# First graph network of a chain: Wm and the two halves of W1 multiplied with each other first, edge sums then on 128 columns

## What is computed

```python
m = max(max(weighting_gate), 0);  exp_e = exp(weighting_gate - m)
row_sum = segment_sum(exp_e, src, num_segments=n_nodes)
atten_e = exp_e / (row_sum[src] + 1e-06)
Mfeat = source_features @ Wm + bm                       # 625 x 512 @ 512 x 256
out0 = segment_sum(atten_e[:, None] * Mfeat[dst], src)  # 625 x 256
out1 = segment_sum(atten_e[:, None] * Mfeat[src], dst)  # 625 x 256
h = concatenate([out0, out1], axis=-1) @ W1 + b1        # 625 x 512 @ 512 x 128
h = relu(layernorm(h, gamma, beta))
h = relu(h @ W2 + b2)                                   # 625 x 128 @ 128 x 512
```

## Time and profile before

| | us |
|---|---|
| median of 3 runs | 2250.25 |
| lowest and highest of them | 2247.23 and 2251.97 |
| the profiled execution, its time | 2255.45 |
| its span, first to last instruction | 2253.6 |
| PE busy | 2119.1 |
| DVE, ACT, POOL busy | 1024.7, 710.9, 551.3 |
| the stretch that the change touches, by PE's rows | 680.7 to 762.1 |

### The profile page before, as it was taken

The page is one execution under the profiler, slowest core; times in us unless marked ns, Lnnn a source line. Parts: engine busy times, 40 slices in busy tenths (PEclk is TensorE's granted clock), DMA queues, the critical chain, the costliest instruction groups (busy, mean ns, idle before and its releaser), DMA issues.

```text
span 2253.6 us, 21932 instructions
## 1 busy us (share of the span) xinstructions
PE 2119.1 (94%) x8162; PEld 1276.7 (57%) x8162; DVE 1024.7 (45%) x2159; ACT 710.9 (32%) x1191; POOL 551.3 (24%) x467
## 2 busy tenths in 40 slices
PE   5899887898889999998999999999999999999998
PEld 3577564787456565554565565565565544444443
DVE  8898677686334324356445355255355300000002
ACT  1477565675231110012242242252251111111110
POOL 4678763453220101012003003002102200122202
PEclk9999999799999789999999999999999899999999
DMA  9522213631112102111011011010101677778832
GB/s 345 178 32 32 27 14 76 171 90 60 41 58 75 38 19 86 43 75 61 15 57 62 19 57 42 30 51 24 53 9 48 246 294 291 295 303 300 300 128 74
DMA packets 61507, 237.47 MB, mean 105 GB/s; under 512 B 23343, under 2 KB 28419, under 8 KB 39276
## 3 DMA queue, kind: packets, MB, share of 16 engines
q1 hardware_dynamic: 31898, 168.25, 20.7%
q0 software_dynamic: 26336, 62.19, 9.0%
q10 hardware_dynamic: 3168, 5.63, 0.7%
HBM read 204.06 MB, written 31.96 MB: 105 GB/s over the span
## 4 chain that ended last, share of the span: by engine, by line
PE 77%; DVE 12%; issue 4%; POOL 3%; ACT 3%; DMA 2%; ACTq 0%; DVEq 0%; POOLq 0%
PE PS L739 10%; PE PS L1027 10%; PE PS L732 9%; PE PS L1420 7%; PE PS L1429 7%; PE PS L1458 7%; PE PS L883 3%; PE PS L1065 3%; PE PS L1306 2%; PE PS L1223 2%; PE PS L1326 2%; PE PS L1327 2%; PE PS L750 1%; PE PS L1205 1%; DVE AR L2436 1%
## 5 line engine op out<-in xcount | busy, mean ns | idle before, releaser
L1984 POOL TENSOR_TENSOR RSTD<-VE,HALF 125x1 f32<-125x1 f32 x100 | 81.1, 811 | 972.5 <-DVE VE L2154 972.5
L1027 PE MATMUL PS<-XT,WR 128*128 128x500 f32 (+2 forms) x992 | 233.5, 392 | 8.4 <-ACT XT L1526 4.4
L883 PE MATMUL PS<-HR,HOT 125*125 125x512 f32 x800 | 211.8, 413 | 16.4 <-DVE HOT L2298 14.9
L2991 DVE TENSOR_TENSOR AR<-AR,PS 128x512 f32<-128x512 f32 (+1 forms) x44 | 30.3, 688 | 404.3 <-PE PS L1429 404.3
L739 PE MATMUL PS<-WR,XT 128*125 128x512 f32 (+1 forms) x464 | 205.5, 590 | 0.6 <-DVE AR L2775 0.3
L1027 PEld LDWEIGHTS PS<-XT,WR 128*128 128x128 f32 x992 | 144.7, 193 | 87.9 <-issue 72.5
L883 PEld LDWEIGHTS PS<-HR,HOT 125*125 125x125 f32 x800 | 147.0, 192 | 58.3 <-DVE HOT L2298 17.2
L2002 POOL DMA_INDIRECT pair_sums<-CW,SIDX x80 | 136.2, 1702 | 54.1 <-DMA pair_sums<-CW,SIDX 21.9
L739 PEld LDWEIGHTS PS<-WR,XT 128*125 128x125 f32 x464 | 86.9, 193 | 89.0 <-issue 85.0
L732 PE MATMUL PS<-XT,WR 128*128 128x313 f32 (+3 forms) x432 | 120.7, 436 | 1.8 <-DVE CW L2262 1.3
L1943 ACT ACTIVATE AR<-PS 128x512 f32<-128x512 f32 (+1 forms) x44 | 26.3, 597 | 299.0 <-PE PS L1420 299.0
(11 more groups left out here) (427 smaller groups left out, 3874.2 us busy)
## 6 DMA issues: line engine op xcount, KB each, us to landing
WR<-in_qkv SPq DMA_DIRECT2D x12, 1024.0 KB
WR<-in_omm SPq DMA_DIRECT2D x12, 1024.0 KB
pair_scores<-CNT SPq DMA_DIRECT2D x1, 12212.0 KB
AR<-pair_scores SPq DMA_DIRECT2D x5, 2187.5 KB
AR<-in_x_a SPq DMA_DIRECT2D x10, 1024.0 KB, 9.8
AR<-in_x_b SPq DMA_DIRECT2D x10, 1024.0 KB, 4.9
AR<-in_x_c SPq DMA_DIRECT2D x10, 1024.0 KB, 7.3
WR<-in_x_a SPq DMA_DIRECT2D x8, 1024.0 KB, 8.9
```

The lines of the kernel that those rows point to most:

```text
L883: last = mm(DIFF[m % 4], HOT[g % 2][0:P, k, tile(j)], HR[0:P, k, :, b, :], start=(k == 0 and b == 0), stop=(k == NT - 1 and b == 1))
L1027: last = mm(by_tile(s)[:, t0:t1, :], w[:, k, 128 * m:128 * (m + 1)], XT[:, k, P * t0:P * t1].rearrange("p (c n) -> p c n", n=P), start=(k ...
L1984: g.tensor_tensor(RSTD[:, t:t + 1], VE[:, t:t + 1], HALF[:, :], ALU.pow)\
```

## The change

Wm and W1 are multiplied with each other before the node features come in: (XT Wm) W1 becomes XT (Wm W1). In part `u` = 2 of the feed-forward network, after the products of `m` = 0, PE turns Wm and the bias row bm (`turn_feature_matrix`, 10 transposes in two W slots). After `m` = 1 it multiplies the turned Wm with both halves of W1 (`joint_weights`): 2 matmuls for the bias row, 8 for the matrix, 256 columns each, in two W slots. ACT copies the four slots to TURNED_WM, JOINT_BIAS and JOINT. `project_narrow` reads JOINT in the place of Wm. The two edge sums are made by node tile, into an N slot for each tile: `hidden_of(t)` is now 10 matmuls of 128 columns with tiles of G and PT as the stationary side and MF moving, and the result stands in node rows. The four turned blocks, their ACT copies and the product with W1 are left out. The product with the noise features (`FW`, 2 matmuls) goes ahead of all `hidden_of`, the waits for the weight batch and for `ROWS` move up into part 2, and DVE waits for JOINT_BIAS before its bias adds.

```diff
+        JOINT = view(XL_, 128, K4, 256)
+        JOINT_BIAS = view(XL_ + K4 * 256, P, 256)
+        TURNED_WM = view(XL_ + K4 * 256 + 256, 128, 2, 640)
...
+            def turn_feature_matrix():
+                weights(0, 3)
+                w_m = WR[:, 0, 0, 0:K4 * 256].rearrange("p (c n) -> p c n", c=K4)
+                pe.wait_ge(rows_in, 16)
+                both = []
+                for k in range(2):
+                    s = fill("W")
+                    for c in range(K4):
+                        nc.tensor.transpose(s.ap[:, 128 * c:128 * (c + 1)], w_m[:, c, 128 * k:128 * (k + 1)], ID[:, :])
+                    nc.tensor.transpose(s.ap[:, D:D + P], ROWS[:, R_BM + 128 * k:R_BM + 128 * (k + 1)], ID[0:P, 0:P])                        .then_inc(s.filled, 1)
+                    both.append((s, n.now(s.filled)))
+                return both
+
+            def joint_weights(turned_wm):
+                w_1 = WR[:, 0, 1, 0:K4 * 128].rearrange("p (c n) -> p c n", c=K4)
+                for half in turned_wm:
+                    copied(half)
+                rows = fill("W")
+                for k in range(2):
+                    last = mm(rows.ap[0:P, 0:256].rearrange("p (a b) -> p a b", a=2),
+                              TURNED_WM[:, k, D:D + P], w_1[:, k::2, :], start=(k == 0), stop=(k == 1))
+                last.then_inc(rows.filled, 1)
+                s = fill("W")
+                for m in range(K4):
+                    for k in range(2):
+                        last = mm(s.ap[:, 256 * m:256 * (m + 1)].rearrange("p (a b) -> p a b", a=2),
+                                  TURNED_WM[:, k, 128 * m:128 * (m + 1)], w_1[:, k::2, :],
+                                  start=(k == 0), stop=(k == 1))
+                last.then_inc(s.filled, 1)
+                return s, n.now(s.filled)
...
+                    if u == 2 and m == 1:
+                        turned_wm = turn_feature_matrix()
+                    if u == m == 2:
+                        joint = joint_weights(turned_wm)
...
+            copied(joint)
             for t in range(NT):
                 copied(turns[t])
-                moved.append(project_narrow(w_m, t, 256))
+                moved.append(project_narrow(JOINT, t, 256))
...
-            sides = [(fill("W"), 2), (fill("W"), 3)]
-            for k in range(NT):
-                pe.wait_ge(moved[k][0].taken, moved[k][1])
-                for s, f in sides:
-                    for c0, c1 in ((0, CUT), (CUT, N)):
-                        last = mm(s.across[0:128, c0:c1], MF[:, k, 128 * (f % 2):128 * (f % 2 + 1)],
-                                  G[:, k, c0:c1], start=(k == 0), stop=(k == NT - 1))
...
-            for f in range(2):
-                s = fill("W")
-                wide(s, 128, NT, lambda k: MF[:, k, 128 * f:128 * (f + 1)], lambda k: PT[:, k, :])
             all_taken("W")
...
-                narrow(s, 128, [(HT[:, f, tile(t)], w_1[:, f, :]) for f in range(4)])
+                terms = [(by[:, k, tile(t)], MF[:, k, 128 * f:128 * (f + 1)], k)
+                         for f, by in ((1, G), (0, PT)) for k in range(NT)]
+                for j, (lhs, rhs, k) in enumerate(terms):
+                    if t == 0 and j < NT:
+                        copied(moved[k])
+                    last = mm(s.ap[0:P, 0:128], lhs, rhs, start=(j == 0), stop=(j == 2 * NT - 1))
+                last.then_inc(s.filled, 1)
```

On ACT the four copies to HT go, and these come:

```diff
+                    if u == 2 and m == 1:
+                        for k in range(2):
+                            s = take("W")
+                            fn(TURNED_WM[:, k, 0:D + P], s.ap[:, 0:D + P], ACT.Copy).then_inc(s.taken, 1)
+                    if u == m == 2:
+                        s = take("W")
+                        fn(JOINT_BIAS, s.ap[0:P, 0:256], ACT.Copy).then_inc(s.taken, 1)
+                        s = take("W")
+                        fn(JOINT[:, :, :], s.ap[:, 0:K4 * 256].rearrange("p (c n) -> p c n", c=K4), ACT.Copy)\
+                            .then_inc(s.taken, 1)
...
-            for f in (2, 3, 0, 1):
-                s = take("W")
-                fn(HT[:, f, :], s.across[:, :], ACT.Copy).then_inc(s.taken, 1)
```

More of the change, by code:

```diff
@@ L1105, in _ @@
                 weights_done()
-            weights(0, 3)
-            w_m = WR[:, 0, 0, 0:K4 * 256].rearrange("p (c n) -> p c n", c=K4)
-            w_1 = WR[:, 0, 1, 0:K4 * 128].rearrange("p (c n) -> p c n", c=K4)
             w_2 = WR[:, 0, 2, 0:D]
             moved = []
+            copied(joint)
             for t in range(NT):
                 copied(turns[t])
-                moved.append(project_narrow(w_m, t, 256))
+                moved.append(project_narrow(JOINT, t, 256))
                 if t < 2:
                     turns.append(turn_tile(3 + t))
-            sides = [(fill("W"), 2), (fill("W"), 3)]
-            for k in range(NT):
-                pe.wait_ge(moved[k][0].taken, moved[k][1])
-                for s, f in sides:
-                    for c0, c1 in ((0, CUT), (CUT, N)):
-                        last = mm(s.across[0:128, c0:c1], MF[:, k, 128 * (f % 2):128 * (f % 2 + 1)],
-                                  G[:, k, c0:c1], start=(k == 0), stop=(k == NT - 1))
-                    if k == NT - 1:
-                        last.then_inc(s.filled, 1)
-            for f in range(2):
-                s = fill("W")
-                wide(s, 128, NT, lambda k: MF[:, k, 128 * f:128 * (f + 1)], lambda k: PT[:, k, :])
             all_taken("W")
@@ L1146, in second @@
                 mm(s.ap[0:P, :], HBT[:, tile(t)], w_2, start=False, stop=True).then_inc(s.filled, 1)
-            hidden_of(0)
-            hidden_of(1)
             s = fill("W")
@@ L1153, in _ @@
             emb_turned = (s, n.now(s.filled))
-            for t in range(2, NT):
+            for t in range(NT):
                 hidden_of(t)
@@ L1158, in _ @@
             wide(s, 128, 1, lambda k: FW[0:16, 16:144], lambda k: ZC)
-            pe.wait_ge(rows_in, 16)
             before = turn_hidden(0)
@@ L1771, in _ @@
             turned_row(4)
-            psum.skip(N=NT)
-            for f in (2, 3, 0, 1):
-                s = take("W")
-                fn(HT[:, f, :], s.across[:, :], ACT.Copy).then_inc(s.taken, 1)
-            psum.skip(N=NT)
+            psum.skip(N=2 * NT)
             s = take("W")
@@ L2569, in _ @@
                     pace = PACE[u][min(m, 1)]
+                    if u == 2 and m == 1:
+                        psum.skip(W=2)
+                    if u == m == 2:
+                        joint_bias = psum.next("W")
+                        psum.skip(W=1)
                     s, k, _ = psum.next("W")
@@ L2586, in _ @@
             dve.wait_ge(rows_in, 16)
+            dve.wait_ge(joint_bias[0].taken, joint_bias[1])
             for t in range(NT):
                 s = take("N")
-                v.tensor_tensor(MF[:, t, :], s.ap[0:P, 0:256], ROWS[:, R_BM:R_BM + 256], ALU.add)\
+                v.tensor_tensor(MF[:, t, :], s.ap[0:P, 0:256], JOINT_BIAS, ALU.add)\
                  .then_inc(s.taken, 1)
-            psum.skip(W=4)
             psum.skip(W=2, T=NT)
```

## The result

| | before | after |
|---|---|---|
| median, us | 2256.98 (20 runs) | 2250.09 (20 runs) |
| lowest, us | 2247.23 | 2239.25 |
| profiled execution, us | 2255.45 | 2243.34 |
| its mean granted clock | 0.972 | 0.972 |

The ratio is 0.9969, with a 95% interval of 0.9958 to 0.9981: by the ratio the changed kernel is faster by 7.0 us, between 4.3 and 9.5. The direction was as forecast and 9.2 us lies inside the interval. The time is not inside the stated range: 2250.09 against 2236 to 2247. The median of before, 2250.25 over the three runs that were shown, is 2256.98 over twenty.

The account below looks back on a forecast made before the run. PE's own work was taken to bound the kernel, with 77% of the chain of waits. Added 17.5 us against 26.66 removed gave 9.2 us less: 2241.0 us from the median 2250.25, range 2236 to 2247.

Parts of the forecast that it names:

- narrow sums: New edge sums on PE: 100 instructions of 128 moving columns, 11.4 us added, with ends 10.4 to 12.6.
- transposes: Ten transposes of 128 or 125 columns on PE, turning Wm and bm: 1.1 us added.
- joint product: Turned Wm and bm times W1 on PE: 20 instructions of 256 columns, 4.3 us added, at most 4.8.
- waits: PE waits for slots in part 2, about 0.5 and 0.2 us: together 0.7 us, between 0 and 1.5.
- Sum of the removed: Old edge sums 10.54 and 10.53, ACT copy wait 0.77, product with W1 2.01 and 2.81: 26.66 us, all on the path.
- The weight batch: PE needs Wm after `m` = 0 of part 2; landed by about 685.5, margin 3.7 us, so no wait.
- the end by the load of the weights alone: Low end for the new edge sums: weight loads bind at 0.104 us an instruction, 10.4 us for 100.
- The band for the clock: One low-clock stretch like the 6 us one at 799 to 805, more or less: 3 us either way.
- The long stretch: Clock 0.50 behind the noise product to 788: 23.4 us costing some 11.7, in both kernels.
- rival 4: Clock stays up as `second` products meet it elsewhere: up to 11.7 us more gain, 2229 to 2236; chance 0.04.
- Rival 2: New edge sums' weight loads not overlapped, or PE waits 4 us or more: 2246 to 2250 us; chance 0.13.
- Rival 3: Clock falls to 0.50 at the `hidden_of` tiles, doubling their time: loss of 4.6 us, 2255; chance 0.03.

## Why the prediction was right and wrong

**The sum was right.** Each term against its measurement: narrow sums 11.4 against 11.11; transposes 1.1 against 0.54 for the first half and 0.77 for the second, which has its start behind the wait in it, together 1.3; joint product 4.3 against 0.86 and 3.72, 4.6; waits 0.7 against 0.41 on DVE between the halves, and less than 0.1 ahead of the joint product. From end to end the additions took 6.33 (6.1 forecast). Sum of the removed: 26.66. Net 9.2 forecast, 9.21 measured in the place. That the two agree to 0.01 is luck: four terms were off by 0.2 or 0.3 us each, and the errors cancel. The jump between two blocks of the moving side costs nothing to speak of. The weight batch was there in time: there is no wait on it. The narrow instructions behaved as the row of the unbroken run had it (0.111 each, against 0.112), and the end by the load of the weights alone, 0.104, was not reached. The estimate of 10.4 us from the Trainium skill ("TensorE: Matmul & The Clock Gate", section on LDWEIGHTS) is 0.7 below what was measured: at this width the load alone does not set the time.

**The level was wrong**, and this is the step of the prediction that failed: "That execution lies 5.2 above the median of the runs shown; with the median 2250.25 it is 2241.0." The sum was made against an execution of 2255.45 us, and I moved it down to a median of three runs. Over twenty runs the median of before is 2256.98 and over 29 it is 2256.32, and the profiled execution was the typical one. Left at its own level, the forecast was 2246.3. With the range's own width, 5 down and 6 up, it would have been 2241 to 2252 and held the 2250.09, which is 3.8 above 2246.3. Whether the three low runs were the scatter of single runs or the level of their session stays open.

**The band for the clock was mis-sized.** I gave it 3 us either way, from one neighbouring stretch of 6 us that may be there or not. The runs of one program spread over 15 us, with many short low stretches ahead of the change and behind it that come and go. The long stretch itself, which I counted "in both kernels", went from 17 to 27 us in the profiles of the two. In one of the nine profiles that have the one-row products it was absent. That is rival 4, of which I had said "Nothing in the trace speaks for it but that the place moves"; it came with longer sums and not with the change. The half-width should have come from the three given runs and the profiled one, which already differ by 8.2 us (2247.23 to 2255.45).

**The gain in the medians** is 6.9, 7.9 and 9.3 us in the three comparisons; by their ratios 7.0, 7.9 and 7.9. At full clock it is 9.1 and 9.3 in the two later jobs. Rival 2 (the gain goes to the weight loads) did not happen: 0.111 a piece. Rival 3 (the clock falls at the narrow sums) did not either: 1.00 over 740 to 752. The prediction had the saving "carried to the end one for one, unless the clock or a wait gives it back". No wait did. The clock probably gave some back: the mean clock was lower by 0.0011 and 0.0006 in the two jobs that have both kernels, which would be 2.5 and 1.4 us, and by 0.0013 with the noise product moved. Together that is nearly three times its error, and of the size of the 1 to 2 us that are missing. Why the change should do this is open. The edit that could have explained it, the place of the noise product, does not.

## What to carry to other kernels

A product of two weight matrices made once can pay when both products stand on TensorE's path: here 4.6 us of joint product, 1.3 of turning and 0.4 of waiting bought 15.5 us of edge sums and second product. Put the sums in the order in which the next engine can take them; turned sums cost the same on TensorE and lost nearly half of the gain in the place to waits, single starts and clock. Before a number is given as a time, look at how much single runs of the unchanged kernel differ, and keep the profiled execution's level if only a few others are known.

## What the runs showed of the hardware

- The same instructions ran at a granted clock of 0.50 for 24 us in five of nine profiled executions, for 17 to 27 us in three more and at 1.00 throughout in one, behind the same kinds of work and with TensorE busy nearly all the time (21.87 of 23 us in after). The Trainium skill ("TensorE: Matmul & The Clock Gate", section on the clock gate) ties the low state to an idle engine. In before and after the engine was busy ahead of this fall (9.37 of 9.40 us in before, 754.9 to 764.3, and 15.00 of 15 in after, 740 to 755), and only the kernel with turned sums had short waits there (0.28 to 1.21 us). The mean clock of a run went from 0.965 to 0.979 over the 12 runs of before with only the added part; a straight line through the runs of a kernel gives 0.5 to 2.5 us for each 0.001.
- Thin products (one row of 125 columns' weights, 512 moving) cost TensorE as much as full ones, 1.05 us a pair at full clock and 2.00 at low. Taking five of them away gave 6 us with DVE. With POOL in the place of TensorE it gave 12 to 13 (2235.95 against the 2248.53 of the changed kernel with only the noise product moved, in the same job), of which the trace shows 6 in the place.
- A float32 matmul instruction with 125 weight columns and 128 moving ones took 0.109 to 0.111 us in long chains. With 65 moving it had been 0.104. That would fit a moving side that begins to add to the time somewhere between 65 and 128 columns; no run changed the width alone.
- Two blocks of 128 columns, 256 apart, as the moving side ran like one block of 256: 16 instructions in 3.72 us, 0.23 each with the start, against 0.216 in a chain of 24.
